# Attention scores of two heads for one tile of rows in one product of 512 columns

## What is computed

```python
x = L0(x, theta, phi)              # rotates pairs of channels
x = L1(x, expert_idx, ...)         # an expert MLP 256-1024-256, chosen per sequence, and a layer norm
x = L2(x, condition, ...)          # one of three small MLPs, chosen per sequence, and a layer norm
# L3: a transformer layer, 16 heads of 16 channels
x = ln(x) * (1 + scale) + shift
q, k, v = x @ Wq + bq, x @ Wk + bk, x @ Wv + bv        # each split into 16 heads
scores = einsum('bhqd,bhkd->bhqk', q / sqrt(16), k) + attention_bias   # bias: 32 x 16 x 256 x 256
scores = where(mask, -inf, scores)
ctx = einsum('bhqk,bhkd->bhqd', softmax(scores), v)
x = x + ctx @ Wo + bo
x = x + gelu2((ln(x) * g2 + beta2) @ W1 + b1) @ W2 + b2
```

## Time and profile before

| what | value |
|---|---|
| median of 3 runs | 2120.6 us (2117.53 to 2122.37) |
| the profiled execution | 2116.27 us, its span 2114.5 us |
| granted clock of TensorE, mean | 0.98 |
| busy: TensorE matmul / weight load | 1939.1 us (92%) / 1681.8 us (80%) |
| busy: VectorE / ScalarE / GpSimd | 75% / 65% / 12% |
| DMA | 356.12 MB in all, hardware queue's packets 54.5% of 16 engines' time |

### The profile page before, as it was taken

How to read it: one execution, slowest core, us unless ns; L and a number is a source line. 1 busy time by engine, 2 the same in 40 slices (tenths; PEclk the granted TensorE clock), 3 DMA queues, 4 the chain that set the end, 5 groups by cost and what they waited for, 6 DMA issues and landing times.

```text
span 2114.5 us, 43618 instructions
## 1 busy us (share of the span) xinstructions
PE 1939.1 (92%) x14354; PEld 1681.8 (80%) x14354; DVE 1587.6 (75%) x5373; ACT 1379.4 (65%) x2211; POOL 252.9 (12%) x361
## 2 busy tenths in 40 slices
PE   5779999999999999999999999999999999999776
PEld 4667888888888888888888888888888888888655
DVE  4467877788787788887777887777878877777763
ACT  3266676677677667667677667766776676677432
POOL 1111110111110011111011111101111110111100
PEclk8699999999999999999999999999999999999997
DMA  6555555656554556555565555566565545654430
GB/s 221 164 167 170 165 144 181 196 185 192 162 176 130 187 185 192 180 177 148 160 191 180 186 170 173 155 183 196 186 192 179 173 149 166 197 180 140 144 101 11
DMA packets 222311, 356.12 MB, mean 168 GB/s; under 512 B 29523, under 2 KB 120147, under 8 KB 222068
## 3 DMA queue, kind: packets, MB, share of 16 engines
q1 hardware_dynamic: 222068, 352.99, 54.5%
HBM read 294.12 MB, written 58.79 MB: 167 GB/s over the span
## 4 chain that ended last, share of the span: by engine, by line
PE 69%; DVE 19%; issue 7%; ACT 3%; DMA 1%; ACTq 0%; POOL 0%; SPq 0%; DVEq 0%; POOLq 0%
PE pD L442 45%; PE pX L658 12%; PE pS L442 9%; DVE bias_ring L1149 8%; DVE bias_ring L946 5%; PE pC L442 1%; DVE x_nat L943 1%; PE pC L680 1%; DVE crossed L943 1%; ACT gelu_out L748 1%; DMA out<-res 1%; ACT L748 1%; ACT probs L748 1%; ACT hid L748 0%; DVE ctx_nat L943 0%
## 5 line engine op out<-in xcount | busy, mean ns | idle before, releaser
L1149 DVE CUSTOM_DVE_ANT_0 bias_ring<-pS,bias_ring 128x256 f32<-128x256 f32 x1024 | 389.6, 418 | 224.1 <-PE pS L442 223.0
L748 ACT ACTIVATE probs<-pX 128x512 f32<-128x512 f32 x512 | 304.4, 594 | 233.9 <-PE pX L658 231.8
L748 ACT ACT_TABLE_LOAD x342 | 438.8, 1283 | 21.7 <-PE pD L442 15.1
L658 PE MATMUL pX<-ident,bias_ring 128*128 128x128 f32 x2048 | 324.1, 281 | 94.7 <-DVE bias_ring L946 76.9
L658 PEld LDWEIGHTS pX<-ident,bias_ring 128*128 128x128 f32 x2048 | 227.1, 141 | 197.8 <-DVE bias_ring L946 188.8
L946 DVE TENSOR_SCALAR bias_ring<-bias_ring,row_max 128x256 f32<-128x256 f32 x1024 | 316.6, 352 | 18.3
L442 PE MATMUL pS<-k_stack,q_stack 96*128 96x256 f32 x1024 | 303.2, 378 | 0.0
L442 PE MATMUL pD<-x,raw 128*128 128x256 f32 x1024 | 249.7, 388 | 5.1 <-ACT gelu_out L748 2.6
L442 PE MATMUL pD<-raw,gelu_out 128*128 128x256 f32 x1024 | 237.3, 380 | 0.0
L442 PEld LDWEIGHTS pD<-x,raw 128*128 128x128 f32 x1024 | 190.5, 193 | 30.6 <-issue 7.4
L442 PEld LDWEIGHTS pS<-k_stack,q_stack 96*128 96x128 f32 x1024 | 196.9, 192 | 19.6
(11 more groups left out here) (148 smaller groups left out, 3680.2 us busy)
## 6 DMA issues: line engine op xcount, KB each, us to landing
bias_ring<-in_fside SPq DMA_DIRECT2D x512, 256.0 KB, 4.0
raw<-in_experts SPq DMA_DIRECT2D x128, 512.0 KB, 4.5
q_spill<-hid SPq DMA_DIRECT2D x96, 256.0 KB, 3.4
k_spill<-hid SPq DMA_DIRECT2D x96, 256.0 KB, 3.4
q_stack<-q_spill SPq DMA_DIRECT2D x128, 192.0 KB, 4.0
k_stack<-k_spill SPq DMA_DIRECT2D x64, 384.0 KB, 5.6
norm<-in_expert_rows SPq DMA_DIRECT2D x32, 384.0 KB, 4.1
x_nat<-in_x SPq DMA_DIRECT2D x32, 256.0 KB, 3.1
```

The lines of the kernel that those rows point to most:

```text
L658: last = e.transpose(pX[:, k, t * P:(t + 1) * P], bias_ring[:, u % NBIAS, t, k * P:(k + 1) * P], ident[:, :])
L748: return e.activation(o, i, func, bias=bias, scale=scale)
L1149: e.tensor_tensor_reduce(bias_ring[:, n, t, :], pS[:, t, :], bias_ring[:, n, t, :], 1.0, -3.4e38, ALU.add, ALU.max, row_max[:, n, t:t + 1] ...
```

## The change

A unit becomes one tile of 128 rows of two heads: t = h % 2 is now the tile, and the pair is g = h // 2 as before. The order, the number of units and the sets of four units that `values` takes stay as they are.

- k_stack takes over the doubled layout with zeros, q_stack the single one. The cleared tile and the three loads per part change accordingly.
- `scores`: the mask product reads the tile's 256 columns twice (a broadcast over the two heads); then one product with 96 x 128 of q_stack as weights and 96 x 512 of k_stack as the moving operand, instead of two with 256 columns.
- `maxima`, `turn`: the same instructions, now indexed by head in place of tile.
- `exponentials`: the output goes to two buffers of probs (one per head), into the columns of tile t, so four runs of 128 elements.
- probs has 6 buffers instead of 5, and bias_ring 6 instead of 7.
- The bias comes from the host in the order of the new units.

```diff
-                    g, par, u = h // 2, h % 2, u0 + h
+                    g, t, u = h // 2, h % 2, u0 + h
...
-                    mm(pS[:, :, :], eye_bf[:, :], mask_add[:, b % 2, :, :], True, False)
-                    for t in range(T):
-                        last = mm(pS[:, t, :], q_stack[:, g, par, t * P:(t + 1) * P], k_stack[:, g, :], False, True)
-                    last.then_inc(sem["scored"], 1)
+                    mm(pS[:, :, :], eye_bf[:, :], mask_add[:, b % 2, t, :].unsqueeze(1).to_broadcast([P, 2, S]), True, False)
+                    mm(pS[:, :, :], q_stack[:, g, t * P:(t + 1) * P], k_stack[:, g, :, :], False, True).then_inc(sem["scored"], 1)
...
-        q_stack = sb("q_stack", [2 * ROWS, NPAIR, 2, S], F32R)
-        k_stack = sb("k_stack", [2 * ROWS, NPAIR, S], F32R)
-
-        NBIAS, NPROBS = 7, 5
+        q_stack = sb("q_stack", [2 * ROWS, NPAIR, S], F32R)
+        k_stack = sb("k_stack", [2 * ROWS, NPAIR, 2, S], F32R)
+
+        NBIAS, NPROBS = 6, 6
...
-                        load(f32(q_stack[own, g0:g1, par, :]), rows[0][own], f"dma_stack{part}")
-                    load(f32(k_stack[:, g0:g1, :]), rows[1], f"dma_stack{part}")
+                        load(f32(k_stack[own, g0:g1, par, :]), rows[1][own], f"dma_stack{part}")
+                    load(f32(q_stack[:, g0:g1, :]), rows[0], f"dma_stack{part}")
...
+                    n, t = u // 2 * 2 % NPROBS, u % 2
                     if u >= NPROBS:
-                        e.wait_ge(sem["valued"], (u - NPROBS) // 4 + 1)
-                    act(flat(probs[:, u % NPROBS, :, :]), flat(pX[:, :, :]), ACT.Exp).then_inc(sem["exp_made"], 1)
+                        e.wait_ge(sem["valued"], (u // 2 * 2 - NPROBS) // 4 + 1)
+                    act(probs[:, n:n + 2, :, t * P:(t + 1) * P], pX[:, :, :].rearrange("p a (k c) -> p a k c", k=K),
+                        ACT.Exp).then_inc(sem["exp_made"], 1)
```

More of the change, by code:

```diff
@@ L56 @@
     "dma_x", "dma_chosen", "dma_norm1", "dma_norm3", "dma_brow", "dma_mask", "dma_out", "dma_spill", "dma_raw0", "dma_raw1", "dma_raw2", "dma_raw3", "dma_stack0",
-    "dma_stack1", *(f"dma_bias{n}" for n in range(7)),
+    "dma_stack1", *(f"dma_bias{n}" for n in range(6)),
     "dve_wide", "dve_front", "dve_sum1", "dve_sum2", "x0_made", "x0_biased", "x0_turned", "x0_copied", "wide_in", "wide_gelu", "wide_out",
@@ L196, in slots @@
             return [flat(tile[:, n:n + 2, :, :].rearrange("p a b c -> p a (b c)")) for n in range(0, tile.shape[1] - 1, 2)]
-        staging = [*slots(probs), *(slots(bias_ring)[n] for n in (2, 0, 1))]
+        staging = [*slots(probs)[0:2], *(slots(bias_ring)[n] for n in (2, 0, 1))]
         NSTAGE = len(staging)
@@ L655, in turn @@
                         e.wait_ge(sem["exp_made"], u)
-                    for t in range(T):
+                    for par in range(2):
                         for k in range(K):
-                            last = e.transpose(pX[:, k, t * P:(t + 1) * P], bias_ring[:, u % NBIAS, t, k * P:(k + 1) * P], ident[:, :])
+                            last = e.transpose(pX[:, par, k * P:(k + 1) * P], bias_ring[:, u % NBIAS, par, k * P:(k + 1) * P], ident[:, :])
                     last.then_inc(sem["turned"], 1)
@@ L1147, in maxima @@
                     e.wait_ge(sem[f"dma_bias{n}"], 16 * (u // NBIAS + 1))
-                    for t in range(T):
+                    for par in range(2):
                         e.tensor_tensor_reduce(
-                            bias_ring[:, n, t, :], pS[:, t, :], bias_ring[:, n, t, :], 1.0, -3.4e38,
-                            ALU.add, ALU.max, row_max[:, n, t:t + 1]).then_inc(sem["max_made"], 1)
+                            bias_ring[:, n, par, :], pS[:, par, :], bias_ring[:, n, par, :], 1.0, -3.4e38,
+                            ALU.add, ALU.max, row_max[:, n, par:par + 1]).then_inc(sem["max_made"], 1)
                     e.wait_ge(sem["max_made"], 2 * u + 2)
-                    for t in range(T):
-                        last = ts(bias_ring[:, n, t, :], bias_ring[:, n, t, :], row_max[:, n, t:t + 1], ALU.subtract)
+                    for par in range(2):
+                        last = ts(bias_ring[:, n, par, :], bias_ring[:, n, par, :], row_max[:, n, par:par + 1], ALU.subtract)
                     last.then_inc(sem["subtracted"], 1)
@@ L1228, in gpsimd_program @@
                     (v_aug[:, :, :, :, HD:HD + 1].rearrange("p a b c d -> p (a b c) d"), 1.0), (minus_half[:, :], -0.5),
-                    (f32(flat(q_stack[:, :, :, :].rearrange("p a b c -> p a (b c)"))), 0.0))):
+                    (f32(flat(k_stack[:, :, :, :].rearrange("p a b c -> p a (b c)"))), 0.0))):
                 e.memset(to, value).then_inc(sem["pool_set"], 1)
@@ L1294, in by_rows, with by_tiles @@
         return a.reshape(*a.shape[:-2], n // P, P, h).swapaxes(-3, -2).reshape(*a.shape[:-2], P, n // P * h)
+    def by_tiles(a):
+        n, heads, rows, c = a.shape
+        return a.reshape(n, heads // 2, 2, rows // P, P, c).transpose(0, 1, 3, 4, 2, 5).reshape(n, heads, P, 2 * c)
     def turned(a):
@@ L1325, in layouts @@
         "ada": by_rows(v["L3_cond_W_ada"]),
-        "x": by_rows(v["x"]), "fside": by_rows(v["fside_Bx16xSxS_0"]), "mask": by_rows(v["mask_Bx1xSxS_bk0"][:, 0]),
+        "x": by_rows(v["x"]), "fside": by_tiles(v["fside_Bx16xSxS_0"]), "mask": by_rows(v["mask_Bx1xSxS_bk0"][:, 0]),
     }
```

## The result

The changed kernel takes 2199.1 us (median of four runs, 2194.2 to 2199.9), the kernel before 2119.6 us beside it: a ratio of 1.0369, 95% interval 1.0349 to 1.0389. It is 3.7% slower. The forecast was 2190 us, and its range, 2163 to 2220, holds the time.

What follows compares the result with a forecast made beforehand. The prediction took TensorE, busy for 92% of the span, as the bound. It summed -9 us (product) and +78 us (28 late biases) to +69 on 2116.3, so 2185, about 2190 us on the median; range 2163 to 2220.

Steps and rivals of the forecast that it cites:

- The load behind SP's stop: SP's queue: unit 4's bias load now first behind the long stop, late in 28 sequences, +78 us.
- The product: TensorE's scores: one product of 512 columns replaces two of 256, saving 0.02 us in each of 512 units; counted -9 us.
- I take about 0.22: TensorE's wide fp32r score product: about 0.22 us, between bounds of 0.21 (bf16 product) and 0.24 (present pair).
- nearly all of it is on the path: TensorE's queue: of the 10 us the product saves, 9 us count in the kernel's time.
- What was costed at nothing: Broadcast mask read, exponentials writing four runs of 128, stack loads, sixth probs buffer: no cost expected.
- The sum: Whole kernel: -9 (product) + 78 (28 late biases) = +69 us.
- rival (d): TensorE: wide product gives nothing or the broadcast read eats it; +78, so 2199 us; 0.78 together with the forecast.
- rival (a): TensorE's clock falls in the new gaps, up to 1.7 us each; 28 give +48, so 2238 us; in full 0.09.
- The sign: TensorE's granted clock: the prediction called itself wrong if it left 1.00 before 1900.
- (b): Only TensorE's own wait at unit 4 counts: 1.5 us per stall, 42 in all; +33, so 2154 us; chance 0.08.
- (c): Unit 4's bias lands in time, no one waits, only the product is left: -9, so 2112 us; chance 0.04.

Runs made afterwards that it cites:

- the one with the stepped bf16 product: The mended order, with the wide score product reading only the upper halves of its fp32r operands as bf16, step of two; 2119.2 us, ratio 0.9990.
- the one with the step moved: Kernel before with all 7 bias buffers, one attention step in SP's order moved from ahead of the expert loads to behind the output; 2199.1 us, ratio 1.0360.
- the mended order: Changed kernel, still 6 bias buffers, one attention step in SP's order moved ahead of the expert loads and output; 2120.1 us, ratio 0.9984 to the kernel before.

## Why the prediction was right, point by point

**The load behind SP's stop.** Right in mechanism, place, number and, within some 4 us, in size. There are 28 waits, 83.9 us against the 82.3 summed from the trace of before; the longest 4.3 against 4.5. TensorE's share at unit 4 was put at 1.1 us and was 0.98; at unit 5 it was 1.43 against 1.5 to 2. That the wait passes through VectorE's queue is shown by the chain; that next to nothing gives it back, by the whole cost of 82 us for 83.9 us of waits. Three pairs of kernels give the worth of the late load: +75 and +76 us in the kernel before, +82 in the new units, of waits of 80.3, 84.3 and 83.9 us. So 5, 8 and 2 us of the waits cost nothing, against the 4.4 us that I let VectorE's idle time absorb. Why these differ is open; the intervals of the ratios (0.2% to either side, 4 us) would nearly cover it.

**The product.** Right in sign, wrong in size: -9 us forecast, -3.4 measured for all of the change but the load (interval -5.7 to -1.3). Two terms of the sum were too large. The first is "I take about 0.22": the wide product costs 0.234, close to the bound of 0.24 that I had given and not to the bf16 row. What the pair had over 0.21 isn't a cost of each weight load, as I had reasoned: of the 0.023 us by which the pair is above 0.216, 0.018 stayed when one load went, and 0.016 of these went when the moving operand was read packed. Most of it is a cost of each column. The second is "nearly all of it is on the path": 0.69 of it is. TensorE's share of the chain in the earlier trace rows is the same number, but one run doesn't show that the two belong together. With both, 512 x 5 ns x 0.69 = 1.8 us. The Trainium skill ("TensorE: Matmul & The Clock Gate", section Back-to-back issue gap) had it nearer with its 1.3 us, though by other parts: its 216 ns hold here for the mask product and nearly for the packed bf16 product (218), not for the fp32r one (234).

**What was costed at nothing.** The broadcast read: the mask product ends 0.216 us after what is before it, as before the change. The exponentials: 593 ns against 594. The stack loads and probs: no new wait names them. The mask and the score product together take 0.450 us against 0.455 before, where the prediction wanted 0.43 against 0.45. VectorE's wait for the scores hardly moved (222.3 us against 223.0), where it was to become somewhat smaller.

**The sum.** +69 forecast, +79.5 between the medians, +83.6 between the two profiled spans. About 6 of the missing 10 us are the product's, and 4 the load's (82 against 78). That is rival (d), product nearly nothing and load in full, which was counted with the forecast and gave 2199.

**The clock, rival (a).** In part. The prediction had named as a sign of being wrong that the clock leaves 1.00 before 1900, and it did. The granted clock, which was 1.00 all through from 106.8 to 1977.3, fell to 0.50 six times in the middle of the changed kernel's profiled run (111.9 to 2047.2), each time for 3.4 us. The first fall, at 163.2, stands ahead of the first late load (193.0). It isn't owed to the late loads: the kernel with the mask added twice has one at 163.3, and the one with the stepped bf16 product at 159.4, and no bias load is late in either. The other five begin 3 to 9 us after VectorE took up its work behind a late load, and their five waits are among the six longest of the 28 (3.7 to 4.3 us). One of them (length, busy us by engine, then the clock; TensorE's is the first):

```profile
852.60:856.00 3.40, 3.40 (x17) 3.20 (x16) 3.30 (x10) 1.47 (x3) 0.00 (x0) 0.50 0.61 156
843.00:852.60 9.60, 5.71 (x48) 3.99 (x47) 8.53 (x25) 2.75 (x6) 2.12 (x3) 1.00 0.70 259
```

TensorE was busy for 5.71 of the 9.60 us before, around one of the long waits (3.7 us), and the clock then stood at 1.2 GHz. The estimate of busy time in rival (a), 6.5 of 9.4, was for an average stall. At most 1.7 us each, the five are worth up to 9 us, an estimate. The kernel before with a ring of 6 had one such fall and +75 us, the one with the step moved six, four of them behind late loads, and +76, so I can't show that they cost anything near that. The sign doesn't overturn the forecast's mechanism, since the late loads bring +75 us with a single fall; it was put too tightly. The Trainium skill's warning ("TensorE: Matmul & The Clock Gate", section HAM oscillation) holds in kind: five falls come behind the gaps, in 5 of 28 rounds.

**Rivals (b) and (c)** are refuted: (b) by the 82 us that the mended order gave back, where it allowed 42, and (c) by the 28 waits and by the landing, 3.99 us in the chain above against 4.0 to 6.4 in the earlier trace rows.

## What to carry to other kernels

When a ring of load buffers gets shorter, look up which load then stands first behind each long stop of the queue that issues it, and compare its landing with the time at which its consumer is ready: that the loads are usually 10 to 20 us ahead said nothing, one unit in sixteen decided. Here the cheap remedy was the place of the load in the queue's order, not the buffer. And before two narrow products are merged, see whether the excess over the ideal belongs to the instruction or to the column: only the first kind is saved.

## What was not expected of the hardware

The time of a product depended on how its moving operand lies in memory. The distances in medians over the units of a trace, nearly all of them at 2.4 GHz:

| moving operand | columns | distance |
|---|---|---|
| bf16, packed (mask, rows broadcast over two heads) | 512 | 0.216 us |
| bf16, packed (k, first 512 bytes of each row) | 512 | 0.218 us |
| bf16, every second half-word (k) | 512 | 0.229 us |
| fp32r (k) | 512 | 0.234 us |
| fp32r (k), as two products | 2 x 256 | 0.121 + 0.118 us |

The fp32r distance of the wide product spread from 0.228 to 0.240 us (10th to 90th percentile), that of the packed bf16 from 0.217 to 0.219. In both bf16 rows of k the weights were bf16 too. What makes the four-byte step slower wasn't tried further.
